# A first attention whose layer norm is folded into its weights, a second norm on ScalarE, and an update in fp32r

## What is computed

```python
mod = (silu(c) @ wmod).reshape(4, 6, 1, 512)          # sa, ca, ga, sb, cb, gb for each batch
ga, gb = sign(g) * max(|g|, 0.25)                      # for both gates
h = layernorm(x) * (1 + ca) + sa
q = einsum('bsD,Ddh->bsdh', h, Wq) + bq                # 16 wide, 32 heads; k and v: one head, 16 wide
scores = einsum('bsdh,bse->bsde', q, k) / 4             # sums over the heads h: 16 x 16 per token
p = softmax(scores, axis=-1)
o = einsum('bsde,bse->bsd', p, v)                      # 16 numbers per token, repeated 32 times
x = x + ga * repeat(o, 32)
h = layernorm(x) * (1 + cb) + sb
x = x + gb * clustered_linear(h)                       # dense 512 x 512, and a softmax over 64 centroids that masks
```

## Time and profile before

| what | value |
|---|---|
| median of 3 runs | 1811.09 us (1808.51 to 1811.34) |
| profiled execution, its own time | 1810.07 us |
| its span, first to last instruction | 1808.2 us |
| instructions in the span | 28904 |
| TensorE busy | 1778.4 us, 98% of the span |
| granted TensorE clock, mean | 0.996 |

### The profile page before, as it was taken

The page is one execution under the profiler, slowest core; times in us unless marked ns, Lnnn a source line. Parts: engine busy times, 40 slices in busy tenths (PEclk is TensorE's granted clock), DMA queues, the critical chain, the costliest instruction groups (busy, mean ns, idle before and its releaser), DMA issues.

```text
span 1808.2 us, 28904 instructions
## 1 busy us (share of the span) xinstructions
PE 1778.4 (98%) x8799; PEld 1483.5 (82%) x8799; DVE 1269.1 (70%) x2977; ACT 1096.2 (61%) x2648; POOL 438.3 (24%) x431
## 2 busy tenths in 40 slices
PE   6998999999999999999999999999999999999999
PEld 4666888888888888888888888888888878888887
DVE  5897787887777677766677777777777777454532
ACT  6665766666666666766667676666666664342331
POOL 2234404041323324041612123140413132011000
PEclk9899999999999999999999999999999999999999
DMA  9026667677676867687776867676777878213110
GB/s 350 7 82 233 187 186 219 203 203 217 180 226 179 224 194 201 188 264 206 223 219 194 236 184 223 200 217 195 220 218 204 235 193 271 90 45 116 40 31 24
DMA packets 239367, 331.24 MB, mean 183 GB/s; under 512 B 26008, under 2 KB 165528, under 8 KB 238880
## 3 DMA queue, kind: packets, MB, share of 16 engines
q1 hardware_dynamic: 238736, 328.93, 61.2%
q10 hardware_dynamic: 528, 1.05, 0.1%
HBM read 200.39 MB, written 129.50 MB: 182 GB/s over the span
## 4 chain that ended last, share of the span: by engine, by line
PE 95%; DVE 3%; ACT 1%; DMA 1%; issue 1%; POOL 0%; SPq 0%; DVEq 0%; ACTq 0%; POOLq 0%
PE ps L2132 28%; PE ps L2202 19%; PE ps L2185 12%; PE ps L2325 11%; PE ps L2168 10%; PE ps L2310 5%; PE ps L1257 2%; PE ps L2165 1%; PE ps L120 1%; PE ps L1165 1%; PE ps L1172 1%; DMA wm<-in_L_wmod_dram 1%; PE ps L1224 1%; PE ps L1233 0%; PE ps L2374 0%
## 5 line engine op out<-in xcount | busy, mean ns | idle before, releaser
L2132 PE MATMUL ps<-hA,wq 128*128 128x512 f32 x1536 | 378.3, 395 | 0.0
L2202 PE MATMUL ps<-wo,oT 128*128 128x512 f32 x1536 | 366.3, 389 | 0.2 <-DVE acc L2754 0.2
L2202 PEld LDWEIGHTS ps<-wo,oT 128*128 128x128 f32 x1536 | 288.1, 188 | 60.1 <-issue 0.4
L2479 ACT ACTIVATE pt<-pd 128x1280 fp32r<-128x1280 f32 x128 | 162.9, 1273 | 273.4 <-PE ps L2185 237.0
L2132 PEld LDWEIGHTS ps<-hA,wq 128*128 128x128 f32 x1536 | 279.5, 188 | 53.7
L2710 DVE CUSTOM_DVE_ANT_0 ps<-ps,mask 128x384 f32<-128x384 f32 (+7 forms) x512 | 220.6, 484 | 143.7 <-PE ps L2168 139.6
L2461 ACT ACTIVATE probs<-ps,nmax 128x384 f32<-128x384 f32 (+7 forms) x512 | 250.2, 503 | 61.6 <-DVE nmax L2710 59.1
L2469 ACT ACTIVATE probs<-probs,rinv 128x384 f32<-128x384 f32 (+7 forms) x512 | 232.6, 526 | 47.8 <-DVE rinv L2721 47.8
L2730 DVE STREAM_TRANSPOSE tp<-probs 128x384 f32<-128x384 f32 (+3 forms) x512 | 215.4, 478 | 4.4 <-ACT probs L2469 4.4
L2185 PE MATMUL ps<-pt,V 128*128 128x256 f32 (+1 forms) x896 | 216.4, 329 | 1.5 <-DVE oT L2743 0.4
L2738 DVE TENSOR_TENSOR pd<-pd,pt 128x1280 fp32r<-128x1280 f32 x128 | 193.3, 1510 | 2.6 <-ACT pt L2479 2.6
(11 more groups left out here) (268 smaller groups left out, 2739.6 us busy)
## 6 DMA issues: line engine op xcount, KB each, us to landing
turned_blocks<-tp SPq DMA_DIRECT2D x128, 640.0 KB, 3.4
pd<-turned_blocks SPq DMA_DIRECT2D x512, 160.0 KB, 3.5
wq_next<-in_L_attn_w_q_dram SPq DMA_DIRECT2D x16, 1024.0 KB, 7.1
wo_in<-in_L_attn_w_o_dram SPq DMA_DIRECT2D x15, 1024.0 KB, 9.7
turned_weights<-hf_chunk SPq DMA_DIRECT2D x168, 64.0 KB, 2.8
wm<-in_L_wmod_dram SPq DMA_DIRECT2D x4, 2048.0 KB, 15.6
turned_values<-tv SPq DMA_DIRECT2D x32, 256.0 KB, 4.0
xh_m<-turned_weights SPq DMA_DIRECT2D x28, 256.0 KB, 3.8
```

The costliest lines, as they stand in the source:

```text
L2132: last = nc.tensor.matmul(ps[:, bank, :], w[i][:, c, cols], hT[k][:, c, b * S:(b + 1) * S], start=(c == 0 and n == 0), stop=(c == DC - 1 a ...
L2202: last = nc.tensor.matmul(ps[:, bank, :], oT[x_][:, b, h, AT[r] * P:(AT[r] + 1) * P], wo[y_][:, h, :], start=(h == 0 and n == 0), stop=(h ...
L2479: nc.scalar.activation(flat(pt[:]), flat(pd[:, u % 2].bitcast(F32)), ACT.Copy).then_inc(phi_done, 1)
```

## The change

Seven things are done.

1. The first layer norm is no longer applied to the rows. `turn(1, b)` transposes X[b] itself as soon as it is loaded, and ACT copies the chunks unmodulated (`columns_of`). Instead `scale_weights` (DVE) multiplies the 48 columns by 1 + ca for each batch, `sum_weights` (PE) makes minus their column sums, `fold` (DVE) adds them to the matrix of `project`, and `offsets` (PE) makes sa times the weights, to which `add_bias` (DVE) adds the bias. 1/std is applied in `products`, tile by tile.
2. `normal1` is gone. `normal2` moves from DVE to ACT, and DVE's part of it is `inverse2`.
3. The first two modulation vectors change places, and the first four are loaded one at a time (`load_one`), the first of them ahead of X[0]. Vector 1 shares a semaphore with the biases, vector 3 with the centroids and the dense weights.
4. o is stored as high, low, high, zero parts of 16 columns, rounded to fp32r, and the gate as high and low parts, so that `update` is one fp32r product over 64 rows for a tile where it was an fp32 product over 16 rows. `turn_o` turns twice.
5. `spread_gate` (POOL) is two operations of half the size.
6. DVE's list has `statistics1(1)` before `outputs(0)`, `statistics1(2)` after `statistics2(0)`, `statistics1(3)` before `add_outputs(1)`.
7. The lists of PE and ACT change accordingly.

The core of the diff:

```diff
 DVE, the folded weights
+                def scale_weights(batches):
+                    for b in batches:
+                        col = mod[0][:, DC * MOD_CA:DC * MOD_CA + DC, b:b + 1].to_broadcast([P, DC, QKV])
+                        last = nc.vector.scalar_tensor_tensor(wscaled[:, b, :, 0:QKV], col, 1.0, wcat[:, :, 0:QKV], ALU.add, ALU.mult)
+                    last.then_inc(wcat_done, 1)
+                def fold(batches, sums):
+                    dve.wait_ge(first_step, sums)
+                    v = slice(batches[0], batches[-1] + 1)
+                    nc.vector.tensor_tensor(folds[:, v, :], sums_bank[:, v, :], spread_over(same_half[:, 0:QKV], batches), ALU.add) \
+                        .then_inc(folded, 1)
+                def add_bias(batches, made):
+                    dve.wait_ge(first_step, made)
+                    v = slice(batches[0], batches[-1] + 1)
+                    link(nc.vector.tensor_tensor(offs[:, v, :], offs_bank[:, v, :], spread_over(bcat[:], batches), ALU.add))
 DVE, products
-                    link(nc.vector.tensor_tensor(qkv[:], pv, bcat[:].rearrange("p (o k) -> p o k", o=1)
-                                                 .to_broadcast([P, TB, 3 * E0]), ALU.add))
+                    for t in range(TB):
+                        last = nc.vector.scalar_tensor_tensor(qkv[:, t, :], pv[:, t, :], rstd1[:, TB * b + t:TB * b + t + 1],
+                                                              offs[:, b, :], ALU.mult, ALU.add)
 DVE, outputs
-                    nc.vector.tensor_tensor(o_t[:, :, 0:E0], by_tile(2), by_tile(1), ALU.mult).then_inc(o_done, 1)
+                    link(nc.vector.tensor_tensor(red[:, 2], red[:, 2], red[:, 1], ALU.mult))
+                    link(nc.vector.tensor_copy(by_part[:, :, 0:3:2, :], twice))
+                    nc.vector.tensor_tensor(o_t[:, :, E0:2 * E0], by_tile, o_t[:, :, 0:E0].bitcast(F32), ALU.subtract).then_inc(o_done, 1)
 PE
+                def sum_weights(batches):
+                    for c in range(DC):
+                        last = nc.tensor.matmul(sums_bank[:, v, :], pick_sums[:], wscaled[:, v, c, 0:QKV], start=(c == 0), stop=(c == DC - 1))
+                def offsets(batches):
+                    pe.wait_ge(mods_sb, 2)
+                    for b in batches:
+                        for c in range(DC):
+                            shift_of = mod[0][:, DC * MOD_SA + c, b:b + 1].to_broadcast([P, P])
+                            last = nc.tensor.matmul(offs_bank[:, b, :], shift_of, wcat[:, c, 0:QKV], start=(c == 0), stop=(c == DC - 1))
+                    last.then_inc(first_step, 1)
-                        at = slice(QB * t, QB * t + E0)
-                        nc.tensor.matmul(ps[:, BANK_U + t % 2, :], oT_[at, :], G[at, b, :], start=True, stop=True).then_inc(upd_ps, 1)
+                        at = slice(OR * (t % 2), OR * (t % 2) + OR)
+                        nc.tensor.matmul(ps[:, BANK_U + t % 2, :], oT_[at, t // 2, :], G[at, b, :], start=True, stop=True).then_inc(upd_ps, 1)
 PE's list, new
+                make_mod(pe, 0); turn_mod(pe, 0); turn(1, 0); make_mod(pe, 1); columns1(0); turn_mod(pe, 1)
+                sum_weights(range(1)); offsets(range(1)); project(0); turn(1, 1); make_mod(pe, 2); columns1(1)
+                turn_mod(pe, 2); make_mod(pe, 3); sum_weights(range(1, B)); offsets(range(1, B)); turn_mod(pe, 3)
+                project(1); spread_gates(0); turn_weights(0); turn_weights(1); centroids(); turn_weights(2); turn_weights(3)
 DVE's list, new
+                scale_weights(range(1)); scale_weights(range(1, B)); inverse1(0); sum_bias()
+                fold(range(1)); add_bias(range(1)); scores(0); mods(3, 0, MOD_GA, MOD_SB)
+                add_bias(range(1, B)); fold(range(1, B)); statistics1(1); outputs(0); inverse1(1); products(1)
+                add_outputs(0, range(2)); shifted(); add_outputs(0, range(2, 4)); statistics2(0); statistics1(2)
+                inverse2(0); low_bias(); mods(6, 0, MOD_SB, 6); outputs(1); inverse1(2); one_hot(); statistics1(3)
+                add_outputs(1); scores(2); statistics2(1); inverse1(3); outputs(2); inverse2(1); scores(3)
 ACT's list, new
+                copy_rows(1); root2(0); root1(2); copy_mod(5); copy_rows(2); copy_rows(3); exponentials(1)
+                normal2(0); take_mod(5); columns_of(2, range(1, 4)); whole(0, range(1)); copy_mod(6)
...
+                columns_of(3, range(3)); root1(3); exponentials(2)
...
+                copy_rows(6); copy_rows(7); normal2(1); copy_columns2(0); copy_o(2)
 SP
+                load_one(0)
                 load_x(0)
-                load_wm(0)
...
+                load_one(1)
...
+                load_x(1)
+                load_one(2)
                 load_x(2)
+                load_one(3)
```

More of the change, by code:

```diff
@@ L276, in adaln_two_blocks @@
                 wf = sb(early, "wf", [P, DC, D], F32)
+            with ExitStack() as early:
+                wq_in = sb(early, "wq_in", [P, DC, D], F32)
             gb_rows = sb(l0, "gb_rows", [P, B, D], F32)
@@ L688, in first_scalar @@
                 copy_o(0)
-                normal1(2)
                 copy_mod(4)
                 round_bias()
-                modulated1(2, range(1))
+                columns_of(2, range(1))
                 take_mod(4)
@@ L695, in first_scalar @@
                 root2(0)
+                root1(2)
                 copy_mod(5)
-                root1(3)
-                exponentials(1)
-                modulated1(2, range(1, 3))
-                take_mod(5)
                 copy_rows(2)
                 copy_rows(3)
-                modulated1(2, range(3, 4))
+                exponentials(1)
+                normal2(0)
+                take_mod(5)
+                columns_of(2, range(1, 4))
                 whole(0, range(1))
@@ L714, in first_scalar @@
                 rounded(0, range(2, 3))
-                normal1(3)
                 rounded(0, range(3, 4))
                 take_mod(7)
-                modulated1(3, range(3))
+                columns_of(3, range(3))
+                root1(3)
                 exponentials(2)
@@ L722, in first_scalar @@
                 drain(0)
-                modulated1(3, range(3, 4))
+                columns_of(3, range(3, 4))
                 copy_rows(5)
@@ L1022, in first_vector @@
                 statistics1(0)
+                sum_queries()
+                dve.wait_ge(mods_sb, 1)
+                dve.wait_ge(wcat_done, WCAT_SUMMED)
+                scale_weights(range(1))
+                scale_weights(range(1, B))
+                dve.sem_inc(mods_done, 1)
                 inverse1(0)
-                sum_queries()
-                mods(2, 0, MOD_SA, MOD_GA)
-                statistics1(1)
                 sum_bias()
-                inverse1(1)
+                fold(range(1), SUMS_FIRST)
+                add_bias(range(1), OFFS_FIRST)
                 scores(0)
                 mods(3, 0, MOD_GA, MOD_SB)
-                statistics1(2)
+                add_bias(range(1, B), OFFS_REST)
+                fold(range(1, B), SUMS_REST)
+                statistics1(1)
                 outputs(0)
-                inverse1(2)
+                inverse1(1)
                 products(1)
@@ L1038, in first_vector @@
                 statistics2(0)
-                statistics1(3)
-                normal2(0)
+                statistics1(2)
+                inverse2(0)
                 low_bias()
@@ L1043, in first_vector @@
                 outputs(1)
-                inverse1(3)
+                inverse1(2)
                 one_hot()
+                statistics1(3)
                 add_outputs(1)
@@ L1048, in first_vector @@
                 statistics2(1)
+                inverse1(3)
                 outputs(2)
-                normal2(1)
+                inverse2(1)
                 scores(3)
@@ L1057, in first_vector @@
                 statistics2(2)
-                normal2(2)
+                inverse2(2)
                 cluster_hits(0)
@@ L1064, in first_vector @@
                 gate_dense(0, range(1))
-                normal2(3)
+                inverse2(3)
                 gate_dense(0, range(1, 4))
```

214 lines of the change are left out of this document (124 added, 90 removed).

## The result

The changed kernel takes 1822.26 us (median of 4 runs, 1821.16 to 1826.38), the kernel before 1810.94 us beside it: a ratio of 1.0074, 95% interval 1.0058 to 1.0091. It is slower by some 11 us where I forecast some 7, and its time lies 0.3 us above the upper end of the range. The profiled execution is the longest of the four, 1826.38 us with a span of 1824.6.

The account below looks back on a forecast made before the run. Hand-offs between VectorE, ScalarE and TensorE bind up to 60 us, then TensorE's queue. A lag of 9.4 us less 2.4 gives 7.0; 1810.1 + 7.0 = 1817.1 for the profiled execution, predicted 1817.5, range 1806 to 1822.

Parts of the forecast that it names:

- The wait at the second `add_bias`: VectorE, batches 1 to 3: idles 3 us or so for offsets done at 36.8, making `outputs(0)` end 4.6 us late.
- the idle at `mods(6)`: VectorE idles some 6 us from about 61 for `take_mod(5)`, going on 7.0 us late.
- the place and length of `normal2(0)`: ScalarE, behind the exponentials and ahead of `take_mod(5)`: 2.93 us for four tiles, ending near 67 us.
- pairs of update at 0.43 us: TensorE, behind `dots(0)`: a pair falls from 1.06 to 0.46 us; the profile should show 0.25 to 0.5.
- The rival of the hidden wait: Offsets done before VectorE reaches `add_bias` at 33.4, so a lag of only 3.6 us: 1813.5 us, chance 0.21.
- TensorE alone: Rival: TensorE's queue alone decides, `turn(2,0)` no later than 60.84, six update pairs save 3.6 us: 1806.6 us, chance 0.17.
- What comes back: From `dots(0)` on TensorE's list is full, so four shorter update pairs give back 2.4 us: lag 9.4 becomes 7.0.
- The lag at `dots(0)`: TensorE starts `dots(0)` at 97.8 us instead of 88.44: 9.4 us late, the largest lag.
- The table loads of `root1(3)`: ScalarE, between the exponentials of batches 1 and 2: two loads of 1.28 us costed at nothing, 2.6 if uncovered.
- The early chain: TensorE's start: dense weights in at 30.6, `project(0)` done at 25.7, then 11.1 us of queued work, offsets done at 36.8.
- The low clock: Rival: low clock in the start and after the idle before `dots(0)`, 7.0 + 2.7 + 2.0: 1822 us, chance 0.17.
- 1.4 us of drain: ScalarE, ahead of the exponentials: the skill page adds this to a table switch, making later times some 1.4 us later.

Follow-up runs that it names:

- the second profile: The changed kernel profiled again with no edit; that repeat took 1822.84 us, ratio 1.0077 to the kernel before.
- Offsets and normalisation alone: Two runs against the kernel before: only the first normalisation folded, 9.8 us above it; only the second normalisation moved to ScalarE, 7.9 us above it.
- the roots together: The change with `root1(3)` beside `root2(1)` and `inverse1(3)` behind `inverse2(1)`, sparing two table loads: 1820.97 us, ratio 1.0067 to the kernel before.

## Why the prediction was wrong

**The direction and the mechanism were right.** The wait at the second `add_bias` (3 us or so forecast, 3.35 measured, 7.69 in the second profile, where VectorE comes to it sooner), the idle at `mods(6)` (6, and 6.00), the place and length of `normal2(0)`, and pairs of update at 0.43 us all came as put down. Offsets and normalisation alone cost 9.8 and 7.9 us. The rival of the hidden wait is refuted: the wait is in all eight profiles in which the statistics stand behind it, even with the offsets moved ahead of the dense weights (2.27 us). Where they stand ahead of it, it is 4.00 and 4.41 us in two profiles and at most 0.24 in the other four. TensorE alone does not decide either: `turn(2, 0)` comes at 70.5 us, not at 61.

**The step that failed is "What comes back".** I let 2.4 us of update time come back after `dots(0)`; in the two profiles the lag grew there by 1.3 and 1.2 us (from 13.1 and 11.8 at `dots(0)` to 14.4 and 12.9). The saving on the pairs is real, but I had assumed that TensorE's list stays full from there. It is busy 8.5 of 10 us in 100 to 110, and the chain runs over VectorE and ScalarE. The delay is not what emptied it: with the old update the stretch from `dots(0)` to `k_first` takes 73.5 to 73.7 us whether it begins on time or 12 us late, and with the new one 74.4 to 75.0, also in the kernel before. There VectorE was busy 8.6 to 9.4 of 10 us; with shorter products on TensorE and two operations more in each `outputs` it became the one that others wait for. So the new update costs some 0.9 us in this stretch (74.5 against 73.7 in the kernel before), where I had it give back 2.4. This step is worth 3.7 us (2.4 + 1.3) of the 7.4 by which the first block's forecast fell short in the first profile, and 3.6 of 5.9 in the second.

**Terms that were mis-sized.** The lag at `dots(0)`, 13.1 and 11.8 us where the sum has 9.4. The table loads of `root1(3)` at nothing: 1.0 to 2.4 us, and my own condition for it ("if that cover were gone") was the case. The early chain: 36.8 for the offsets, measured 38.8 and 38.9, for two different reasons in the two profiles: the low pace up to 30 us in one, the dense weights at 32.4 and not 30.6 in the other. The 30.6 was read from the old order of the transfers, though the new one issues the weights 2.7 us later or more. What I had not seen is that they set a floor: behind `make_mod(3)`, with the weights in at 32.4, the offsets can't be done before 37.3 even at the full pace (32.4 + 1.06 + 1.0 + 2.8), and the profile of the roots together has them just then; in one where that step began at 31.4 they were done at 36.3. `outputs(0)` itself took 6.1 us where the sum has 5.9, with POOL beside it. Of all this 1.3 us are left at `mods(6)`.

**The low clock** was a rival with 0.17 at 1822, and it came, in part: low pace in the start of the first profile, from 50 to 60 us, and after the idle ahead of `dots(0)` (1.76 and 1.56 us for 1.00). That its number is nearly the measured one is luck: its terms were 2.7 us for the start, of which the first profile has 1.0 at the end of `project(0)` and the second none, and 2.0 behind `dots(0)`, and it kept the 2.4 that did not come back. An episode on a full TensorE was measured at 6 us in the version with the old update, where I had put 2. The Trainium skill, "ScalarE: Activation LUTs", "What ACT_TABLE_LOAD costs", adds 1.4 us of drain; in the change too the load starts 0.02 us behind the copy ahead of it (62.70 + 1.07) and the exponentials 0.02 us behind the load (63.79 + 1.28, 65.09), so the trace shows none. And the overlap of products on different row groups, which the Trainium skill, "TensorE: Matmul & The Clock Gate", states under "Packing small matmuls", isn't seen in the new pair: it takes 0.43 us in the chain, about twice the 0.23 at which the products of `linear` follow each other there (six in 1.38).

**The second block** was taken as unchanged; it was longer by 1.2 and 2.0 us in the profiles of the change.

## What to carry to other kernels

Price a moved step by what stands behind it in its queue, and ask of every new wait which transfer it inherits: here the offsets waited for weights that they don't use, because their place was behind a step that does. Do not book a saving on a full engine before looking at the next one: where that is nearly as full (here 8.6 to 9.4 of 10 us), the saving turns into idle time, and the operations that the change adds there decide. And where a change opens idle time on TensorE, add the clock: afterwards the full stretch may run at half pace, in some executions and not in others.

## What the runs showed of the hardware

- The same kernel with the same instructions had an episode at 1.2 GHz from 105 to 117 us in one execution and not in another, which made it 6 us longer. Over its twelve executions the mean granted clock was 0.991 or 0.992 in the three shortest and 0.986 to 0.989 in the nine others. Six executions lay from 1822.5 to 1834.5, the next six from 1821.6 to 1830.4.
- VectorE's rounding to fp32r of 128 columns takes 0.23 us alone and 1.21 with POOL at work beside it; a subtraction of 64 columns took 0.23 and once 1.31.
- A pair of fp32r products over 64 rows and 512 columns takes 0.43 to 0.50 us at 2.4 GHz, where the pair of fp32 products over 16 rows took 1.06.
- 128x128 weights with 48 fp32 columns: 24 instructions in 2.77 us, 0.12 each, in thirteen profiles, and in 5.19 us in the one with the granted clock at 0.50 there; with 144 columns eight took 1.25.
